# A state-space mixer on one core: a scan over chunk states replaced by products of all chunk pairs

## What is computed

```
proj = hidden @ in_proj_w.T                  # gate 4096 | x 4096, B 1024, C 1024 | dt 64
x, B, C = silu(causal_conv4(x, B, C))        # 64 heads of 64 channels, 8 groups of N = 128
dA = exp(dt * A);  dtx = dt * x
state_t = state_{t-1} * dA_t + dtx_t B_t^T   # per head, 64 x 128
y_t = state_t C_t + D x_t
out = (rmsnorm per 512 channels(y) * norm_weight * silu(gate)) @ out_proj_w.T
```

## Time and profile before

| | us |
|---|---|
| median of 3 runs | 3161.83 (3161.66 to 3165.03) |
| the profiled execution | 3168.56 |
| its span, first to last instruction | 3166.9 |
| PE, PEld, DVE busy | 3087.4, 2533.2, 2423.1 |
| ACT, POOL busy | 1183.5, 469.4 |

### The profile page before, as it was taken

How to read it: one execution, slowest core, us unless ns; L and a number is a source line. 1 busy time by engine, 2 the same in 40 slices (tenths; PEclk the granted TensorE clock), 3 DMA queues, 4 the chain that set the end, 5 groups by cost and what they waited for, 6 DMA issues and landing times. The chain is left out here.

```text
span 3166.9 us, 46751 instructions
## 1 busy us (share of the span) xinstructions
PE 3087.4 (97%) x15048; PEld 2533.2 (80%) x15048; DVE 2423.1 (77%) x4252; ACT 1183.5 (37%) x1890; POOL 469.4 (15%) x515
## 2 busy tenths in 40 slices
PE   7999999999999997999999999999997999999998
PEld 6888888888888886888888888888885888888776
DVE  7777786877787787887877778687876888677877
...
PEclk9999999999999998999999999999998999999999
...
GB/s 129 118 80 87 81 67 87 67 99 64 102 74 79 87 61 128 123 61 103 72 86 83 76 86 67 86 70 96 68 85 93 143 143 145 141 193 216 212 198 173
DMA packets 168068, 335.13 MB, mean 106 GB/s; under 512 B 14193, under 2 KB 84977, under 8 KB 167921
## 3 DMA queue, kind: packets, MB, share of 16 engines
...
q0 software_dynamic: 4096, 14.68, 1.2%
...
## 5 line engine op out<-in xcount | busy, mean ns | idle before, releaser
L876 PE MATMUL bank<-x_hi,w_hi 128*128 128x512 f32 x2560 | 1025.8, 401 | 0.5 <-DVE acc L637 0.5
L878 PE MATMUL bank<-x_hi,w_lo 128*128 128x512 f32 x2560 | 1001.5, 391 | 0.0
L877 PE MATMUL bank<-x_lo,w_hi 128*128 128x512 f32 x2560 | 997.2, 390 | 0.0
L637 DVE SCALAR_TENSOR_TENSOR acc<-bank,conv_w,acc 128x511 f32<-128x511 f32 (+2 forms) x576 | 431.0, 748 | 334.7 <-ACT acc L453 307.9
L878 PEld LDWEIGHTS bank<-x_hi,w_lo 128*128 128x128 f32 x2560 | 480.4, 188 | 105.0
L877 PEld LDWEIGHTS bank<-x_lo,w_hi 128*128 128x128 f32 x2560 | 481.9, 188 | 93.6
L876 PEld LDWEIGHTS bank<-x_hi,w_hi 128*128 128x128 f32 x2560 | 481.4, 188 | 92.7 <-issue 1.3
L1383 PE MATMUL bank<-wo_hi,y_hi 128*128 128x512 f32 x1024 | 402.7, 393 | 26.6 <-DVE wo_lo L1250 23.3
L1384 PE MATMUL bank<-wo_lo,y_hi 128*128 128x512 f32 x1024 | 400.6, 391 | 0.0
L1385 PE MATMUL bank<-wo_hi,y_lo 128*128 128x512 f32 x1024 | 400.4, 391 | 0.0
L453 ACT ACTIVATE acc<-bank,tap_par 128x512 f32<-128x512 f32 x192 | 149.3, 777 | 616.2 <-PE bank L878 594.2
...
## 6 DMA issues: line engine op xcount, KB each, us to landing
w_raw<-in_w_in SPq DMA_DIRECT2D x160, 512.0 KB, 3.6
cum_b<-cum_scratch ACTq DMA_DIRECT2D x128, 512.0 KB, 3.8
y_raw<-y_scratch SPq DMA_DIRECT2D x128, 512.0 KB, 3.4
y_scratch<-gate SPq DMA_DIRECT2D x128, 256.0 KB, 2.4
wo_raw<-in_w_out SPq DMA_DIRECT2D x128, 256.0 KB, 3.5
xbc<-in_x SPq DMA_DIRECT2D x16, 512.0 KB, 3.7
yn<-in_x SPq DMA_DIRECT2D x16, 512.0 KB, 3.7
o_sb<-in_x POOLq DMA_DIRECT2D x16, 512.0 KB, 6.1
```

The lines of the kernel that those rows point to most:

```text
L637: dve.scalar_tensor_tensor(acc[:, s % 2, back:], bank_proj[s % 2][:, 0:SEQ - back], mix.conv_w[:, g, m, 3 - back:4 - back], acc[:, s % 2, ...
L876: pe.matmul(out, w_hi[m % 2][:, k, :], hi, start=(k == 0), stop=False)
L877: pe.matmul(out, w_hi[m % 2][:, k, :], lo, start=False, stop=False)
L878: mm = pe.matmul(out, w_lo[m % 2][:, k, :], hi, start=False, stop=(k == KT - 1))
```

## The change

The carried state is gone. For each pair of chunks of one sequence (source chunk k, later chunk j >= k) the decayed B-C product is made directly and y comes out channel-major:

- The unit of work is a pair of heads (128 channels) of one sequence, 8 units a group, in place of a chunk. `attn` holds for each head the four source chunks against all later tokens: widths 512, 384, 256 and 128, 1280 columns (`SPAN`), in a ring of three buffers.
- `scores`: per sequence four products of B and C with those widths, masked by `masked` on DVE into `bc`. `turn_x`: four turns of x a unit. `mult`: per source chunk and head one product of 64 weight columns (dt x) with 512, 384, 256 or 128 moving columns, the first head written to partitions 0 to 63 of the bank and the second to 64 to 127, accumulated over the chunks. B's own turn, the carried-in and state products and `turn` of y are gone.
- The cumulated decays of all pairs are written to DRAM once a half (1280 per head and sequence), and SP loads 2 heads of one sequence to all partitions for each unit (1.31 MB), in place of 512 KB a chunk on ACT's queue. `exps` is nine ACT instructions per head in place of DVE's differences and one ACT exponential per chunk.
- D x is added with y's read from the bank (`finish_y`). Squares are added up per channel on POOL, summed over channels by PE (`channel_sums`, eight products with one moving column a group), and the reciprocal root goes through DRAM (`rc`) and back to all partitions before POOL multiplies it into the gated y (`scale`, 128x2048), one 1 MB store per sequence.
- The projections come in the order B, C, x, gate. `Plan` gives the slot of each step: `FIRST` for group 0, `LATER` for the rest; slots of 20 and over lie in the next group, or behind the last projection in `drain`.
- In half 0 the prefetch of x comes behind the last group's stores in SP's queue.

The diff, cut to its core (engine by engine: tables, SP, POOL, ACT, DVE, PE):

```diff
+WIDTH = [SEQ - k * P for k in range(CHUNKS)]
+OFFSET = [sum(WIDTH[:k]) for k in range(CHUNKS)]
+SPAN = sum(WIDTH)
...
+RING = 3
...
+ORDER = [XT, XT + 1] + list(range(XT)) + list(range(CONV_TILES, TILES))
...
+class Plan:
+    def __init__(self, cb, load, mult, gate_from):
+        self.cb, self.bc = cb, [s + 1 for s in cb]
+        self.load, self.mult = load, mult
+        self.exp = [s - 3 + h for s in mult for h in range(2)]
+        self.turn = [s - 2 for s in mult]
+        self.attn = [s - 1 for s in mult]
+        self.square = [s + 1 for s in mult]
+        self.gate = [max(s + 1, gate_from + 1 + u) for u, s in enumerate(mult)]
+        self.norm = [s + 2 for s in mult[-SEQS:]]
+        self.var = [s + 3 for s in mult[-SEQS:]]
+        self.rc = [s + 4 for s in mult[-SEQS:]]
+        self.rb = [s + 5 for s in mult[-SEQS:]]
+        self.scale = [s + 6 for s in mult[-SEQS:]]
+        self.store = [s + 7 for s in mult[-SEQS:]]
...
+FIRST = Plan(cb=[9, 10], load=[9, 10, 12, 14, 15, 17, 19, 20], mult=[13, 14, 16, 18, 19, 21, 23, 24],
+             gate_from=CONV_SLOTS)
+LATER = Plan(cb=[4, 6], load=[4, 5, 7, 10, 12, 14, 16, 18], mult=[9, 11, 13, 15, 17, 19, 21, 23],
+             gate_from=CONV_SLOTS)
+DRAIN = max(LATER.store) + 1
...
+            def load_cum(g, u, first):
+                c, q = divmod(u, SEQS)
+                if first and u < RING:
+                    sp.wait_ge(cum_stored, 16)
+                    if u == 1:
+                        sp.wait_ge(summed, 2)
+                    if u == 2:
+                        sp.wait_ge(mix_turned, NT)
+                elif u >= RING:
+                    sp.wait_ge(multiplied, UNITS * g + u - RING + 1)
+                else:
+                    sp.wait_ge(multiplied, UNITS * (g - 1) + max(range(u, UNITS, RING)) + 1)
+                sp.dma_start(attn[u % RING][:, :, :],
+                             d["cum"][half, q, bass.ds(g * HPG + 2 * c, 2), :].partition_broadcast(P)
+                             ).then_inc(cum_loaded[u % RING], 16)
+            def piece(g, plan, s):
+                for u in due(plan.load, s):
+                    load_cum(g, u, plan is FIRST)
+                for q in due(plan.rc, s):
+                    sp.wait_ge(rstd_done, SEQS * g + q + 1)
+                    sp.dma_start(d["rc"][q].rearrange("(p k) -> p k", k=CHUNKS), rstd[:, q, :]).then_inc(rstd_stored[q], 16)
+                for q in due(plan.rb, s):
+                    sp.wait_ge(rstd_stored[q], 16 * (g + 1))
+                    sp.dma_start(rstd_b[:, q, :], d["rc"][q].partition_broadcast(P)).then_inc(rstd_loaded[q], 16)
+                for q in due(plan.store, s):
+                    sp.wait_ge(scaled, SEQS * g + q + 1)
+                    sp.dma_start(d["y"][half, bass.ds(g * XT, XT), :, q * SEQ:(q + 1) * SEQ].rearrange("k p i -> p k i"),
+                                 gate[:, :, q * SEQ:(q + 1) * SEQ]).then_inc(stored[q], 16)
...
+            def gate_y(g, u):
+                c, q = divmod(u, SEQS)
+                part = gate[:, c, q * SEQ:(q + 1) * SEQ]
+                pool.wait_ge(y_done, UNITS * g + u + 1)
+                pool.wait_ge(gate_done, GATE_SLOTS * g + u + 1)
+                pool.tensor_tensor(part, part, y[:, u % 2, :], ALU.mult).then_inc(gated, 1)
+            def add_square(g, u):
+                q = u % SEQS
+                n = ADDS * g + u - SEQS
+                pool.wait_ge(squared, UNITS * g + u + 1)
+                if u >= 2 * SEQS:
+                    pool.wait_ge(added, n - 1)
+                pool.tensor_tensor(sums[:, q, :], sums[:, q, :], sq[:, :], ALU.add).then_inc(added, 1)
+            def rstd_of(g, q):
+                pool.wait_ge(var_done, SEQS * g + q + 1)
+                need(pool, rstd_stored[q], 16 * g)
+                pool.tensor_tensor(rstd[:, q, :], var_eps[:, q, :], core.neg_half[:, 0:CHUNKS],
                                    ALU.pow).then_inc(rstd_done, 1)
+            def scale(g, q):
+                part = gate[:, :, q * SEQ:(q + 1) * SEQ]
+                pool.wait_ge(rstd_loaded[q], 16 * (g + 1))
+                pool.wait_ge(gated, UNITS * g + UNITS - SEQS + q + 1)
+                pool.tensor_tensor(part, part, rstd_b[:, q, :].unsqueeze(1).to_broadcast([P, XT, SEQ]),
+                                   ALU.mult).then_inc(scaled, 1)
...
             groups(sp, step)
+            drain(piece)
             if half + 1 < HALVES:
-                sp.wait_ge(started, NT * GROUPS)
+                sp.wait_ge(y_done, UNITS * GROUPS)
                 prefetch_x(sp, d, mix, half + 1, x_ahead)
...
+            def exps(g, u, h):
+                c, q = divmod(u, SEQS)
+                tile = attn[u % RING][:, h, :]
+                head = bass.ds(g * HPG + 2 * c + h, 1)
+                if h == 0:
+                    act.wait_ge(cum_loaded[u % RING], 16 * (RING_USES[u % RING] * g + u // RING + 1))
+                for k in range(CHUNKS):
+                    part = tile[:, OFFSET[k]:OFFSET[k] + P]
+                    op = act.activation(part, part, ACT.Relu, bias=mix.cum[:, CHUNKS * q + k, head], scale=-1.0)
+                op.then_inc(fall_done, 1)
+                for k in range(CHUNKS - 1):
+                    part = tile[:, OFFSET[k] + P:OFFSET[k] + WIDTH[k]]
+                    act.activation(part, part, ACT.Exp, bias=mix.dec[:, CHUNKS * q + k, head])
+                act.wait_ge(fall_done, 2 * UNITS * g + 2 * u + h + 1)
+                near = tile[:, 0:2 * WIDTH[0]].rearrange("p (a b) -> p a b", b=WIDTH[0])[:, :, 0:P]
+                act.activation(near, near, ACT.Exp, scale=-1.0)
+                step = WIDTH[2]
+                near = tile[:, OFFSET[2] - P:OFFSET[2] - P + 2 * step].rearrange("p (a b) -> p a b", b=step)[:, :, P:step]
+                op = act.activation(near, near, ACT.Exp, scale=-1.0)
+                if h == 1:
+                    op.then_inc(exp_done, 1)
+            def square(g, u):
+                c, q = divmod(u, SEQS)
+                act.wait_ge(y_done, UNITS * g + u + 1)
+                if c == 0:
+                    need(act, normed, SEQS * (g - 1) + q + 1)
+                    out = sums[:, q, :]
+                else:
+                    need(act, added, ADDS * g + u - SEQS)
+                    out = sq[:, :]
+                act.activation(out, y[:, u % 2, :], ACT.Square, scale=GC ** -0.5).then_inc(squared, 1)
...
+            def masked(g, q, first):
+                dve.wait_ge(cb_done, SEQS * g + q + 1)
+                if first and q == 0:
+                    dve.wait_ge(cum_stored, 16)
+                need(dve, multiplied, UNITS * g)
+                for k in range(CHUNKS):
+                    op = dve.tensor_tensor(bc[:, q, OFFSET[k]:OFFSET[k] + WIDTH[k]], cb_out[k],
+                                           core.mask[:, 0:WIDTH[k]], ALU.mult)
+                op.then_inc(bc_done, 1)
+            def weigh(g, u):
+                q = u % SEQS
+                dve.wait_ge(exp_done, UNITS * g + u + 1)
+                dve.wait_ge(bc_done, SEQS * g + q + 1)
+                dve.tensor_tensor(attn[u % RING][:, :, :], attn[u % RING][:, :, :],
+                                  bc[:, q, :].unsqueeze(1).to_broadcast([P, 2, SPAN]), ALU.mult).then_inc(attn_done, 1)
+            def times_dt(g, u):
+                c, q = divmod(u, SEQS)
+                dve.wait_ge(x_turned, UNITS * g + u + 1)
+                need(dve, multiplied, UNITS * g + u - 1)
+                steps = mix.dt[:, CHUNKS * q:CHUNKS * (q + 1), bass.ds(g * HPG + 2 * c, 2)]
+                dve.tensor_tensor(dtx[:, u % 2, :, :].rearrange("p k (h c) -> p k h c", c=HD),
+                                  bank_tr[:, :].rearrange("p (k h c) -> p k h c", h=2, c=HD),
+                                  steps.unsqueeze(3).to_broadcast([P, CHUNKS, 2, HD]), ALU.mult).then_inc(dtx_done, 1)
+            def finish_y(g, u, first):
+                c, q = divmod(u, SEQS)
+                dve.wait_ge(multiplied, UNITS * g + u + 1)
+                if first and u < 2:
+                    for i in range(2):
+                        dve.wait_ge(branch_stored[i], 16 * NT // 2)
+                need(dve, squared, UNITS * g + u - 1)
+                need(dve, gated, UNITS * g + u - 1)
+                dve.scalar_tensor_tensor(y[:, u % 2, :], xbc[:, c, q * SEQ:(q + 1) * SEQ],
+                                         mix.d_ch[:, bass.ds(g * XT + c, 1)], bank_y[u % 2][:, :],
+                                         ALU.mult, ALU.add).then_inc(y_done, 1)
+            def variance(g, q):
+                dve.wait_ge(normed, SEQS * g + q + 1)
+                need(dve, rstd_done, SEQS * (g - 1) + q + 1)
+                dve.tensor_scalar(var_eps[:, q, :], bank_y[q][:, 0:CHUNKS],
+                                  NORM_EPS, None, ALU.add).then_inc(var_done, 1)
...
+            def scores(g, q):
+                pe.wait_ge(silu_done, CONV_SLOTS * g + SEQS + q + 1)
+                need(pe, bc_done, SEQS * g + q)
```

(43 more changed lines are left out.)

527 lines of the change are left out of this document (197 added, 330 removed).

## The result

The changed kernel takes **3202.9 us** (median of four runs, 3201.0 to 3210.9) against 3163.4 us for the kernel before in the same comparison: a ratio of 1.0127, with a 95% interval of 1.0106 to 1.0148. The forecast was 3186, so the sign was right and the loss 39.5 us where I had 24. The profiled execution took 3210.9 us, its span 3209.4 us against 3166.9. It is the longest of the four; the others took 3201.0 to 3203.1 us, at a mean granted clock of 0.977 to 0.978 where it had 0.975.

A forecast was written before the change was run, and what follows sets the result against it. The prediction took PE to bound each group, and a chain over all engines the ends of the halves. Body -31 us, ends +52 and group 0 +3 gave +24 us, so 3186 us, with a range of 3130 to 3440.

The forecast's parts named there:

- What bounds it: Inside a group PE's work lies end to end; only work added to or taken from PE moves its 143.4 us.
- The part removed: PE's old products and turns in a group, 33.2 us, against 31.5 added: 1.7 us less a group.
- The product: `mult` on PE: two heads overlap, but staggered, 2.73 us a unit and 21.8 a group.
- the rival that I gave 0.16: `mult` passes pack without stagger: 2.28 us a unit, 5.3 us less a group, 3124 in all; chance 0.16.
- changing to and from this form costs nothing: On PE, going between full products and those with 64 weight columns brings no pause: 0 us.
- The channel sums: Eight PE products with one moving column, priced from the 128x64 product at 0.22 each: 1.7 us a group.
- a rival at 1.7 us a group: POOL's `scale` around slots 7 and 8 holds up DVE, so PE stands; 27 us in all, 3213; chance 0.08.
- Group 0: ACT's larger table, 12 more PE turns and two heads' exponentials in slots 11 and 16: +3 us for both halves.
- The last groups: Each half's last group, part of whose work lies behind the last projection, gains 3.6 us: -7 in all.
- The ends: Behind each half's last projection the chain takes 46 us: +23 a half, +6 for half 0's prefetch, +52 in all.
- the stagger: In `mult`, PE starts products in order and one head's two passes follow each other on the same half: 2.73 us a unit.
- the fast rival: `mult` passes pack without stagger, 2.28 us a unit; body -86, ends +48, group 0 at 0: 3124; chance 0.16.

The follow-up runs named there:

- e1: The changed kernel with `mult`'s loops swapped, all four products of one head before the other's: 3379.0 us (one run).
- e5: The changed kernel with ACT storing the squares by phase, so that the channel sums' weights are neighbours and `scale` keeps its form: 3167.5 us, ratio 1.0008.
- e2: The changed kernel with the channel sums' weights taken as neighbours and POOL's `scale` reading the roots in steps of four: 3190.2 us, ratio 1.0085.
- b1: The changed kernel with squares by phase, group 0's second scores a slot later and the prefetch before the way through DRAM: 3147.6 us, ratio 0.9947.
- b5: b4 with the last group's products of units 4 to 7 in slots 16, 17, 19 and 20: 3105.8 us, ratio 0.9807.
- e3: The changed kernel with group 0's second scores in slot 11 instead of 10: 3177.2 us, ratio 1.0045.
- b4: b1 with every `scale` on DVE instead of POOL, at the end of slots 9 and 11 (10 and 11 behind group 0): 3127.1 us, ratio 0.9873.

## Why the forecast held, and where its steps failed

**What bounds it** was right: a group is PE end to end. The part removed, 33.2 us, can be checked with what is measured now: 22.7 for `mult` and turns (8 x (2.31 + 0.53)), 4.1 for the scores and 3.7 for the sums make 30.5, so 2.7 less, and 1.0 more for POOL: 1.7 less; measured 2.2 (143.9 to 141.7). (The 143.4 of the earlier trace rows was the length of the window; from start to start a group took 143.9, so that the forecast's 141.7 is met partly by luck.)

**The product** failed in its mechanism. The step "PE starts its products in order, and the two passes of one head follow each other on the same half" gave 2.73 us. The pairs of starts and e1 show that each half takes its own products as it comes free; a unit takes 2.31, the 2.28 of the rival that I gave 0.16. That rival's price held and its total didn't: the terms below took the gain away. A second step failed beside it: that the earlier trace rows "show that changing to and from this form costs nothing". Each change costs 0.17 us, so the turns of x take 0.53 a unit where a product of `mult` follows, and not 0.43, and the unit 2.31 where the scores' widths alone are 2.07. The Trainium skill, "TensorEngine Tiling (Array Packing)", Key Properties, says that tiles work in parallel, and the trace agrees (5 to 7 ns between the starts); it says too that a change of the tiling mode drains the engine, which I left aside in the prediction, and the 0.17 us a change fit it in kind, though no run takes them apart. The 2.9 us that I estimated from the Trainium skill, "TensorE: Matmul & The Clock Gate", Part 3, was too much.

**The channel sums** were mis-sized: 1.7 us a group from the 128x64 product, measured 3.7. The bounds "between 0 and that" were wrong on the upper side, because I looked only at the number of columns; the weights are read in steps of four. With neighbours the sums cost about what I had: e5 takes 1.8 us a group off, 25 us over the 14 groups that hold sums.

**The clock** inside a group had no term at all. Behind the sums of slot 3 it falls for 3.4 us, 1.6 us a time, 9 times in the profile: 14 us. What PE does before it is the unit's 16 passes and then eight passes of one column whose loads take 326 ns each; with loads of 199 to 201 ns it falls behind the sums in none of seven profiles (e2, e5, b1 to b5). That points to the loads, but they alone do not decide: with the slow ones it falls in 2 of 14 groups of e1, and in e3's other executions hardly at all.

**POOL** I costed at nothing for DVE, with a rival at 1.7 us a group and 27 in all, chance 0.08. It is there, 1.0 us a group: b4 won 15.5 us by taking it away. The step that failed is "while DVE's L676 stays within 1.211 to 1.223, so I cost POOL's new work at nothing": there L345 began behind L676 wherever they met. The place was another as well: the first `scale`, in slot 7, costs PE nothing, and the second, which starts late in slot 9, lengthens slots 10 and 11. `scale` takes 4.6 us, and my 3.7 came from 1024 columns. The Trainium skill, "SBUF — State Buffer", section "SBUF: two separate sides", says that whichever of the two engines starts second blocks, DVE where it has two SBUF inputs; here DVE's 4.76 us beside POOL's 4.59 agree, and so do the steps of the convolution, which have one and are not held. I should have let that rule, which the rows showed from one side only, carry a term.

**Group 0** had +3 us for both halves. Its wait and the fall of the clock behind it cost 15.3 us (e3), as the plan asks for the second scores in the slot in which `masked` of the first still stands behind a convolution. I listed ACT's table and PE's turns there, and not who empties the banks of the scores.

**The last groups** should have given 3.6 us each, and in the table group 7 gave 0.3. That is mostly the table's cut. Of the work that I put behind the last projection, only 3.3 us of the old and 3.2 of the new (my prices) are missing in group 7; the rest is missing in group 0, which has no group ahead of it. Cut like the table, the forecast is -8 us for groups 0 and 1 and -3 for group 7. Group 7 is then 2.5 us too long, of which two falls of the clock are 3.2, and groups 0 and 1 are 14 us too long, which is group 0's wait.

**The ends**: +52 forecast, +46.4 measured. In half 0 each step is within 2.1 us, and the total within 0.6. In half 1 the next phase's first DMA is issued 45.7 us behind the last projection (forecast 46) and was 24.0 before (I took 22.5 for both). The rest is in the last phase itself, which ran 4.0 us shorter (740.0 to 736.0 us). In the other variants, which do not touch it, it took 732.6 to 737.1; none of these runs tells why.

The forecast's 3186 is thus 17 us low. By the spans it is 18.5: the groups are 24 us longer than forecast, the ends 6 shorter. In the groups, what I had too high (the stagger, 0.42 x 8 x 16 = 54 us; the scores, 7) met what I had too low or not at all (the turns 13, the sums 28, POOL 14). These are 61 us against 55, and that they nearly cancel is luck; with group 0's wait (15) and the clock (14) they come to 23. With the product's price right alone, the forecast would have been near the fast rival's 3124, farther off than 3186.
